# Epsilon and the gate columns' difference on POOL, and the copies of the second weights one slot later

## What is computed

```python
def _layernorm(x, axis=-1, eps=1e-05):
    m = jnp.mean(x, axis=axis, keepdims=True)
    v = jnp.var(x, axis=axis, keepdims=True)
    return (x - m) / jnp.sqrt(v + eps)
...
    def _L0_xattn_ref(q, k, v, gamma):
        ...
        qk = jnp.einsum('bhdq,bhdl->bhql', qh, kh) * scale
        sm = jax.nn.softmax(qk, axis=-1)
        ret = jnp.einsum('bhql,bhdl->bhdq', sm, vh)
        ...
    def _L0_ffn_ref(x, Wg, W0a, b0a, W0b, b0b, W1a, b1a, W1b, b1b):
        ...
        top_expert = jnp.argmax(scores, axis=-1)
        h0 = jax.nn.gelu(jnp.einsum('bsh,fh->bsf', x, W0a) + b0a, approximate=False)
        out0 = jnp.einsum('bsf,hf->bsh', h0, W0b) + b0b
        h1 = jax.nn.relu(jnp.einsum('bsh,fh->bsf', x, W1a) + b1a)
        out1 = jnp.einsum('bsf,hf->bsh', h1, W1b) + b1b
        ...
    x = x + _L0_xattn_ref(_layernorm(x, axis=-1), ctx_2048, ctx_2048, L0_xattn_gamma)
    x = x + _L0_ffn_ref(_layernorm(x, axis=-1), ...)
```

## Time and profile before

| | us |
|---|---|
| median of 3 runs | 228.93 |
| lowest, highest | 228.88, 229.73 |
| profiled execution | 228.8 |
| its span, first to last instruction | 227.0 |
| PE busy | 216.2 (95%) |
| DVE busy | 174.5 (77%) |
| ACT busy | 146.3 (64%) |
| POOL busy | 137.8 (61%) |

### The profile page before, as it was taken

The page is one execution under the profiler, slowest core; times in us unless marked ns, Lnnn a source line. Parts: engine busy times, 40 slices in busy tenths (PEclk is TensorE's granted clock), DMA queues, the critical chain, the costliest instruction groups (busy, mean ns, idle before and its releaser), DMA issues.

```text
span 227.0 us, 5325 instructions
## 1 busy us (share of the span) xinstructions
PE 216.2 (95%) x2036; PEld 166.0 (73%) x2041; DVE 174.5 (77%) x357; ACT 146.3 (64%) x220; POOL 137.8 (61%) x180
## 2 busy tenths in 40 slices
PE   7889897888999999999999999999999999999995
PEld 2334454446786888788787978787878886989994
DVE  7499987999679976997699959996688734446683
ACT  6204766876985597857785769559755877745240
POOL 6752313979889717973689348961865187555720
PEclk9999999999999999999999999999999999999999
DMA  4695499644224350626052712423112000000101
GB/s 139 222 332 197 107 353 388 226 143 143 94 67 173 83 178 6 230 68 221 4 163 95 226 35 77 140 83 132 29 48 74 0 27 3 23 26 0 49 1 46
DMA packets 19393, 26.40 MB, mean 116 GB/s; under 512 B 1992, under 2 KB 12840, under 8 KB 19112
## 3 DMA queue, kind: packets, MB, share of 16 engines
q1 hardware_dynamic: 18942, 25.66, 34.4%
q10 hardware_dynamic: 426, 0.40, 0.5%
HBM read 11.01 MB, written 2.10 MB: 58 GB/s over the span
## 4 chain that ended last, share of the span: by engine, by line
PE 78%; DVE 9%; DMA 4%; ACT 4%; issue 3%; POOL 1%; SPq 0%
PE ff L782 21%; PE ff L802 13%; PE od L729 11%; PE st L717 11%; PE ff L814 7%; PE smax L704 5%; DVE nmax L396 4%; PE od L737 3%; ACT P L578 2%; DMA qkst<-mlow 2%; PE od L744 2%; PE tr L755 2%; PE od L686 2%; PE tr L765 2%; DMA qkst<-parts 1%
## 5 line engine op out<-in xcount | busy, mean ns | idle before, releaser
L578 ACT ACTIVATE P<-st 128x1024 f32<-128x1024 f32 x64 | 66.2, 1034 | 39.3 <-PE st L717 38.7
L396 DVE TENSOR_REDUCE nmax<-smax 128x4 f32<-128x1024 f32 x54 | 65.9, 1221 | 16.1 <-PE smax L704 15.1
L267 POOL TENSOR_TENSOR mv<-mv,power 128x1 f32<-128x1 f32 x32 | 19.0, 595 | 47.9 <-DVE mv L378 47.8
L782 PE MATMUL ff<-xnTh,w1h 128*128 128x256 f32 x128 | 38.7, 302 | 0.0
L782 PE MATMUL ff<-xnTh,w1l 128*128 128x256 f32 x128 | 36.0, 281 | 0.0
L782 PE MATMUL ff<-xnTl,w1h 128*128 128x256 f32 x128 | 35.8, 280 | 0.0
L285 POOL TENSOR_TENSOR hidL<-hid,hidH 128x1024 fp32r<-128x1024 f32 x13 | 31.0, 2386 | 6.7 <-DVE hidH L457 5.3
L717 PE MATMUL st<-qkst 64*128 64x256 f32 x256 | 32.2, 330 | 2.4 <-DMA qkst<-mlow 1.4
L611 ACT ACTIVATE hid<-ff,b1t 128x256 f32<-128x256 f32 x64 | 26.1, 479 | 10.8 <-PE ff L782 10.7
L802 PE MATMUL ff<-w2h,hidH 128*128 128x256 f32 x124 | 32.0, 291 | 0.0
L729 PE MATMUL od<-P,vt 128*32 128x256 f32 x512 | 30.9, 382 | 0.0
(11 more groups left out here) (81 smaller groups left out, 373.8 us busy)
## 6 DMA issues: line engine op xcount, KB each, us to landing
qkst<-parts SPq DMA_DIRECT2D x47, 256.0 KB
xv<-in_xv SPq DMA_DIRECT2D x16, 256.0 KB, 2.9
qk<-in_qk SPq DMA_DIRECT2D x15, 256.0 KB, 3.5
out<-y SPq DMA_DIRECT2D x16, 128.0 KB, 2.6
w1t<-in_w SPq DMA_DIRECT2D x1, 1024.0 KB, 7.2
w2t<-in_w SPq DMA_DIRECT2D x1, 1024.0 KB, 7.9
qkst<-parts ACTq DMA_DIRECT2D x1, 256.0 KB
qkst<-mlow SPq DMA_DIRECT2D x16, 8.0 KB
```

Of the source, the lines that this page charges most:

```text
L267: pool.tensor_tensor(mv[:, b % 2, 11:12], mv[:, b % 2, 10:11], power[:, 0:1], ALU.pow).then_inc(s_rstd, 1)
L396: dve.tensor_reduce(nmax[:, c % 2, :, :, j].rearrange("p a e -> p e a"), (ff if c in WIDE and j % 2 else smax)[:, :, :, :], AX.X, ALU.max, ...
L578: act.activation(P[:, b % 2, j, :, :, :].rearrange("p e a l -> p (e a l)"), st[:, :, :, :].rearrange("p e a l -> p (e a l)"), ACT.Exp, sca ...
L782: mm = pe.matmul(ff[:, u // 2 % 2, u % 2, :], w[:, a, e, m * 128:(m + 1) * 128], xs[:, i % 2, a, :], start=a == 0 and n == 0, stop=a == LC ...
```

## The change

POOL adds epsilon, by an instruction of its own in `rstd`, and waits for its result before it takes the root; VectorE signals after the aggregate. At the start POOL takes the root of batch 1 behind both low parts of batch 0 and no longer ahead of them. The difference of the gate columns is made by POOL in slot 6. ScalarE makes the two copies of the second weights in slots 13 and 14 in place of 12 and 13, and behind the copy of the values where that is in the same slot; POOL's low parts of these weights go to slots 13 to 16.

```diff
@@ rstd on POOL
-            def rstd(b, mv, count, s_var, s_rstd):
+            def rstd(b, mv, count, s_var, s_eps, s_rstd):
                 pool.wait_ge(s_var, count)
+                pool.tensor_scalar(mv[:, b % 2, 10:11], mv[:, b % 2, 9:10], EPS, None, ALU.add).then_inc(s_eps, 1)
+                pool.wait_ge(s_eps, count)
                 pool.tensor_tensor(mv[:, b % 2, 11:12], mv[:, b % 2, 10:11], power[:, 0:1], ALU.pow).then_inc(s_rstd, 1)
@@ the start of POOL
-            rstd(0, mv1, 1, s_var1, s_rstd1)
-            rstd(1, mv1, 2, s_var1, s_rstd1)
+            rstd(0, mv1, 1, s_var1, s_eps1, s_rstd1)
             pool.wait_ge(s_k0hi, 1)
             pool.tensor_tensor(parts[:, 0, 3, :], qk[:, 0, 1, :], parts[:, 0, 2, :], ALU.subtract).then_inc(s_k0lo, 1)
             pool.wait_ge(s_hi, 1)
             pool.tensor_tensor(parts[:, 0, 0, :], qk[:, 0, 0, :], parts[:, 0, 1, :], ALU.subtract).then_inc(s_lo, 1)
+            rstd(1, mv1, 2, s_var1, s_eps1, s_rstd1)
             low(1)
-            rstd(2, mv1, 3, s_var1, s_rstd1)
+            rstd(2, mv1, 3, s_var1, s_eps1, s_rstd1)
@@ the loop of POOL
                 if j == 2 and b >= 3:
                     add_bias(b - 3)
+                if n == 6:
+                    pool.wait_ge(s_small, 32)
+                    pool.tensor_tensor(wgd[:, :], wgb[:, 0, :], wgb[:, 1, :], ALU.subtract).then_inc(s_wgd, 1)
...
-                if 12 <= n < 16:
-                    units = slice(2 * (n - 12), 2 * (n - 11))
-                    pool.wait_ge(s_w2h, (n - 12) // 2 + 1)
+                if 13 <= n < 17:
+                    units = slice(2 * (n - 13), 2 * (n - 12))
+                    pool.wait_ge(s_w2h, (n - 13) // 2 + 1)
                     pool.tensor_tensor(w2l[:, units, :], w2t[:, units, :], w2h[:, units, :], ALU.subtract).then_inc(s_w2l, 1)
@@ VectorE
-                dve.bn_aggr(m[:, 8:10], m[:, 0:6]).then_inc(s_aggr, 1)
-                dve.wait_ge(s_aggr, count)
-                dve.tensor_scalar_add(m[:, 10:11], m[:, 9:10], EPS).then_inc(s_var, 1)
+                dve.bn_aggr(m[:, 8:10], m[:, 0:6]).then_inc(s_var, 1)
...
                 if b == 0:
-                    dve.tensor_tensor(wgd[:, :], wgb[:, 0, :], wgb[:, 1, :], ALU.subtract).then_inc(s_wgd, 1)
                     dve.wait_ge(s_wgd, 1)
@@ the loop of ScalarE
-                if n in (12, 13):
-                    act.wait_ge(s_w2, 16)
-                    half = slice((n - 12) * HM, (n - 11) * HM)
-                    act.activation(w2h[:, half, :], w2t[:, half, :], ACT.Copy).then_inc(s_w2h, 1)
                 if j == 2 and b >= 1:
                     copy_od(b - 1)
                     if b >= 4 and b % 2 == 0:
                         for u in range(4, 8):
                             hidden((b - 4) // 2, u)
+                if n in (13, 14):
+                    act.wait_ge(s_w2, 16)
+                    half = slice((n - 13) * HM, (n - 12) * HM)
+                    act.activation(w2h[:, half, :], w2t[:, half, :], ACT.Copy).then_inc(s_w2h, 1)
```

More of the change, by code:

```diff
@@ L132, in build @@
         s_fill = [sem(f"s_fill{n}") for n in range(4)]
-        s_stat1, s_aggr1, s_var1, s_rstd1, s_qn = map(sem, ("s_stat1", "s_aggr1", "s_var1", "s_rstd1", "s_qn"))
+        s_stat1, s_var1, s_eps1, s_rstd1, s_qn = map(sem, ("s_stat1", "s_var1", "s_eps1", "s_rstd1", "s_qn"))
         s_hi, s_lo, s_q0, s_k0hi, s_k0lo = map(sem, ("s_hi", "s_lo", "s_q0", "s_k0hi", "s_k0lo"))
@@ L138, in build @@
             sem, ("s_ods", "s_odT", "s_rden", "s_attT", "s_aT", "s_x1"))
-        s_stat2, s_aggr2, s_var2, s_rstd2, s_xn = map(sem, ("s_stat2", "s_aggr2", "s_var2", "s_rstd2", "s_xn"))
+        s_stat2, s_var2, s_eps2, s_rstd2, s_xn = map(sem, ("s_stat2", "s_var2", "s_eps2", "s_rstd2", "s_xn"))
         s_lead, s_mask, s_chosen, s_xb = map(sem, ("s_lead", "s_mask", "s_chosen", "s_xb"))
@@ L332, in _ @@
                 for c in prepared(n):
-                    rstd(c, mv1, c + 1, s_var1, s_rstd1)
+                    rstd(c, mv1, c + 1, s_var1, s_eps1, s_rstd1)
                 if j == 0 and b >= 5 and b % 2:
@@ L346, in _ @@
                 if j == 0 and b >= 2:
-                    rstd(b - 2, mv2, b - 1, s_var2, s_rstd2)
+                    rstd(b - 2, mv2, b - 1, s_var2, s_eps2, s_rstd2)
                 if j == 2 and b >= 2:
@@ L356, in _ @@
                     pool.tensor_tensor(w1l[:, half, e, :], w1t[:, half, e, :], w1h[:, half, e, :], ALU.subtract).then_inc(s_w1l, 1)
-                if 12 <= n < 16:
-                    units = slice(2 * (n - 12), 2 * (n - 11))
-                    pool.wait_ge(s_w2h, (n - 12) // 2 + 1)
+                if 13 <= n < 17:
+                    units = slice(2 * (n - 13), 2 * (n - 12))
+                    pool.wait_ge(s_w2h, (n - 13) // 2 + 1)
                     pool.tensor_tensor(w2l[:, units, :], w2t[:, units, :], w2h[:, units, :], ALU.subtract).then_inc(s_w2l, 1)
-            rstd(B - 2, mv2, B - 1, s_var2, s_rstd2)
+            rstd(B - 2, mv2, B - 1, s_var2, s_eps2, s_rstd2)
             masks(B - 2)
@@ L364, in _ @@
             low_hidden(LAST - 1, 0)
-            rstd(B - 1, mv2, B, s_var2, s_rstd2)
+            rstd(B - 1, mv2, B, s_var2, s_eps2, s_rstd2)
             masks(B - 1)
@@ L371, in _, with moments @@
         def _(dve):
-            def moments(b, src, mv, count, s_stat, s_aggr, s_var):
+            def moments(b, src, mv, count, s_stat, s_var):
                 m = mv[:, b % 2, :]
@@ L384, in moments1 @@
                     dve.wait_ge(s_qk[place(c, QK)], 16 * turn(c, QK))
-                moments(c, qk[:, place(c, QK), 0, :], mv1, c + 1, s_stat1, s_aggr1, s_var1)
+                moments(c, qk[:, place(c, QK), 0, :], mv1, c + 1, s_stat1, s_var1)
             def q_norm(c):
@@ L427, in moments2 @@
                 dve.wait_ge(s_x1, b + 1)
-                moments(b, x1[:, b % X1, :], mv2, b + 1, s_stat2, s_aggr2, s_var2)
+                moments(b, x1[:, b % X1, :], mv2, b + 1, s_stat2, s_var2)
             def x_norm(b):
```

## The result

| | before | after |
|---|---|---|
| median | 228.88 us (9 runs) | 230.32 us (9 runs) |
| lowest, highest | 228.68, 229.73 | 229.99, 231.7 |
| ratio, with its 95% interval | | 1.0067 (1.0046 to 1.0088) |
| profiled execution, span | 227.0 us | 228.5 us |

A forecast was written before the change was run, and what follows sets the result against it. It took TensorE to bound the kernel from 55 us, and before that a chain of waits and a full VectorE. Profiled 228.8 us, plus 0.81 at the start, minus 0.62 in the middle, gave 229.0 us, range 227.9 to 229.9.

The forecast's parts named there:

- The start: Up to batch 0's first row maximum on VectorE: claimed at 11.65 instead of 10.84 us, 0.81 us later.
- a delay at 10.84 should come through whole: At batch 0's first maximum: claimed that transposition, scores and weight traffic all wait behind it, so the full 0.81 us counts.
- 36 to 55 us: Stretch where VectorE is full, ahead of the first FFN product: claimed 0.62 us earlier, bounds 0 and 1.18.
- VectorE's share: In 36 to 55 us: add and aggregate wait leave VectorE, 0.21 us saved for each of four moments.
- The gate columns: In 36 to 55 us: their subtraction leaves VectorE, saving 0.34 us; on POOL, in slot 6, costed at nothing.
- The copies: In 36 to 55 us: ScalarE's second weights copy, behind the copy of the values, claimed to cost 0.56 us.
- The first FFN product: Beginning of TensorE's steady stream: claimed near 55.35 us, against 55.16 before.
- Zero: After 55 us: claimed no loss, since extra POOL work takes 0.3 of 0.94 us idle before the hidden layer's low half.
- signs of being wrong: First maximum by 11.0, FFN product outside 54.2 to 56.2, no idle POOL before low halves, post-55 stretch off over 0.3 us.
- that pair: At the start: VectorE's normalise beside POOL's low part, claimed to take 0.81 us where the median is 0.39.
- Nothing for the time: POOL's low parts of the second weights in slots 13 to 16: claimed no cost, first reader in slot 19.
- The one that ended slower: Steady part: POOL becomes last for TensorE, 1.2 us of work against 0.94 us of cover; 230.6 us, chance 0.07.

The follow-up runs named there:

- n_eps_only: Kernel before with epsilon left out everywhere: VectorE's addition and its wait gone, none on POOL; 228.01 us, ratio 0.9950.

## Why the prediction was wrong, step by step

- **The start: the mechanism was right, the term too large.** Of 0.81 us forecast at the first maximum 0.85 were there. It went on as if the delay came through whole, and 0.56 arrived at slot 8. The step that failed is "a delay at 10.84 should come through whole": the four maxima are 0.17 us shorter when their inputs are ready (4.63 against 4.80), and 0.1 went in the row transfer. Undoing the order gave back 0.37 in the trace: a start that is earlier by 0.80 at slot 0 meets SyncE's own list of issues, a limit that the forecast did not have.
- **36 to 55 us: right in what is saved on VectorE, wrong in what comes in its place.** 0.62 were forecast, 0.23 measured. VectorE's share alone is the forecast 0.84 (n_eps_only). Not in the sum were POOL's additions in that same stretch, 0.36. The gate columns were put at 0.34 and brought 0.11. The copies were put at 0.56 and cost 0.36.
- **The first FFN product came nearly as forecast (55.43 against 55.35), by luck.** The start was put 0.25 us too late and the middle 0.39 us too early, and these two errors cancel but for 0.14 (0.33 at slot 17, where they add up to 0.19).
- **After 55 us: "Zero" is the step that broke the forecast.** It was 1.03 us: 0.54 between slots 20 and 21, and 0.49 in three steps. Two of the forecast's own signs of being wrong came: no idle POOL ahead of the low half at 67.01, and a stretch after 55 us longer by over 0.3 us. The forecast looked for idle time of POOL ahead of the low half of the hidden layer (0.94 us) and counted what POOL's work would take of it (0.3). For the three steps idle time is rightly found: even in after POOL idles 0.83 us at 91.44. But there the extra work did not act through POOL's queue. It shifted POOL's additions of the bias until VectorE's normalise fell beside them, and the delay came by VectorE. The forecast knew that pair from the start of the kernel, and applied it only there.
- **The weights' low parts one slot later: "Nothing for the time" was wrong in company.** The forecast looked at their own reader, six slots off, and not at what is queued behind them on POOL. Alone the move costs 0.06 at slot 20; together with the additions 0.54.
- **The rivals.** The one that ended slower named the place, the low half of the hidden layer, but a wrong way there: it wanted 0.94 us of cover used up before anything is lost, and 230.6 us. That the measured 230.32 us lie near its time is chance. With the move of the weights in company, though, POOL's cover was used up at slot 20, and its queue was last: there the rival had the place and the wait right, though it counted the additions alone.
- **What stays open.** Why the row transfer that ends near 36 us took 5.15 us in one trace and up to 5.79 in another, no run here was made for. It moves single traces by as much as a part of the change. For the same reason, and since SyncE's issues can be last ahead of it, it is open how much of the 0.80 us of the order an execution keeps at its end: 0.37 in the one pair of traces, 0.8 by the ratios, whose intervals leave 0.6 to either side.

## What to carry to other kernels

Work that is moved to an engine with idle time is not free where operations of that engine and of the one it came from lengthen each other, as those of POOL and VectorE do here: ask for every operation of the other engine that is on the path whether the shifted work now runs beside it, and whether it ends later. Idle time ahead of a critical operation protects it against a longer queue, not against that. And what is queued behind a moved instruction counts more than who reads its result: two moves that each fit have to be costed together.

## What was not expected of the hardware

- Both sides of such a pair get longer. VectorE's normalise of 0.39 us took 0.45 to 0.96 beside POOL's operations (0.96 at 98.69 in n_eps_only), and its end went by the end of POOL's operation, 0.14 to 0.16 us behind it. POOL's root of one column, 0.55 to 0.57 us alone, took 0.65 to 0.84 beside VectorE's gate product; two additions took 2.08 us instead of 1.55.
- Of an addition of one column on POOL 0.22 us are the operation and 0.07 the wait for its result. The same on VectorE costs 0.21, of which only 0.07 to 0.09 is the addition (its successor starts that much behind it): the rest is the wait for the aggregate, which goes with it.
